# Moving the preparation of latent attention's weights into the opening block of the layer before it

## The chip, the cores and the metric

One Trainium2 chip, one of its cores, with its five engines: TensorE (PE), VectorE (DVE), ScalarE (ACT), GpSimd (POOL) and SyncE (SP), which issues the DMAs. The metric is the device time of one execution in microseconds; lower is better. TensorE's clock is granted at one of two levels, 1.2 or 2.4 GHz; the profile gives it as a share of the upper one.

## The reference

Eight sequences of 512 tokens, 256 wide, go through six sub-layers: an expert feed-forward, a small attention, the expert feed-forward again, a routed layer, latent attention, and the routed layer again. Cut to the two that matter here:

```python
# latent attention: B=8, L=512, D=256, 16 heads of 64, latent 64
x_bld = layernorm(x)
q = einsum('bld,dhk->blhk', x_bld, Wq)
latent = einsum('bld,dc->blc', x_bld, Wkv_down)
k = einsum('blc,chk->blhk', latent, Wk_up)
v = einsum('blc,chk->blhk', latent, Wv_up)
attn = softmax(where(causal, einsum('bqhd,bkhd->bhqk', q, k) / sqrt(64), neg_inf))
x = x + einsum('bqhd,hdo->bqo', einsum('bhqk,bkhd->bqhd', attn, v), Wout)

# routed layer: 64 tokens of each sequence, by the router's weight, 63 of them kept
weights = (layernorm(x) @ router_w)[..., 0] + router_b[0]
topv, topi = top_k(weights, 64); sel_idx = sort(topi[:, :63])
# the chosen tokens go through rmsnorm, rope, attention with a mask, a feed-forward
out = zeros_like(x).at[bidx, sel_idx].set(proc)
x = x + 0.5 * (out + layernorm(x) * (1.0 - sel_mask)[..., None])
```

## The kernel before

`macaron_kernel` calls four layer functions one after the other; x (all tokens, 128 partitions) and the identity matrix stay in SBUF between them. Each layer is a row of blocks; a block is one instruction stream per engine, and all engines meet at its end. `layer` clears the layer's semaphores, one by one on SyncE, in a block of its own after each layer.

`routed_layer` (tag routed1 or routed2) has an opening block and a main block. In the opening block SyncE issues three small loads (router row, router bias, position rows; `small_in`) and nine loads of weights (`weights_in`). VectorE goes through statistics of 32 tiles (L982), the layernorm's columns (`layernorm_columns`, L81 to L61), 32 weighings (L992: x less its mean times the router's row, summed into `w_col`), and waits for TensorE to turn `w_col` into rows (L1055, `rows_turned`). Then it picks the 64 largest of each sequence in 8 rounds (L1017, L1019), numbers them (L1026 to L1044), and copies them back after another turn by TensorE (L1061) to `slot_col` and `stay` (L1046, L1047). ScalarE writes the normalized tokens `y`, 32 tiles in 8 batches (L1072), from when `shift` is there (L985). GpSimd writes a few constants. In the main block TensorE gathers the chosen tokens from `y` with one-hot matrices (L1208), and the layer goes on.

`latent_attention_layer` has two blocks. The first prepares weights. SyncE loads Wk_up, Wv_up, Wq, Wout and Wkv_down (L1681 to L1685); TensorE turns the first three (L1708, L1714) and VectorE copies the turned ones to SBUF (L1751, L1754). Then for each of 8 pairs of heads TensorE multiplies Wq with Wk_up (L1727) and Wv_up with Wout (L1730), so that the layer can work on the latent directly. Each product is needed as a sum of two float16 tiles: ScalarE writes the upper part (`b_hi` L1780, `a_hi` L1781) and VectorE the rest (`b_lo` L1768, `a_lo` L1770), straight from PSUM. GpSimd makes constants, and VectorE fills tiles whose unused rows must be 0 or 1 (L1742 to L1748). The second block is the attention: `stream` walks a pipeline over batches and heads; its first steps are the layernorm of the first batch, with statistics on VectorE (L74), the variance on GpSimd (L111 to L124), the start of the reciprocal root on VectorE (L49), Newton steps on GpSimd (L131 to L137), the normalized tiles on VectorE (L102), then turns on TensorE (L1969).

The order of the work is written out by hand, in each engine's stream; waits name counts of semaphores.

## Time and profile before

| | us |
|---|---|
| median of the runs | 2927.89 (2927.53 to 2929.93, 3 runs) |
| the profiled execution | 2929.78, its span 2928.0 |
| TensorE busy | 2487.5 (85%) |
| VectorE busy | 2105.5 (72%) |
| ScalarE busy | 1570.2 (54%) |
| GpSimd busy | 843.4 (29%) |

The page also divides the span into 40 slices of 73.2 us; a digit is the busy share in tenths (for PEclk, the granted clock). The first expert and attention layers take the first 21 slices and a half; the first routed layer runs from 1585 to 1782 us, latent attention from 1786 to 2717, the second routed layer from there.

```profile
## 2 busy tenths in 40 slices
PE   6999999999999999989995567588888888897276
PEld 3444444444444444444442355255555555564164
DVE  3479688878979896888512754589778878974754
ACT  5655454645555554546553251277667766765241
POOL 3444343444444443435442100002112211212000
PEclk9999999999999999999998766699999999998577
```

The 22nd to 26th digits are the routed layer and the start of latent attention: the lowest digits of TensorE but for the ends, and the lowest clock but for the last layer. Times in the rows further down are microseconds from the start of the span.

### The profile page before, as it was taken

What the parts mean: (1) busy time and instruction counts of PE and PEld (TensorE: products, weight loads), DVE (VectorE), ACT (ScalarE), POOL (GpSimd) and SP (SyncE); (2) the same over time, 40 slices, a digit from 0 to 9 for tenths busy, and PEclk for the clock granted to TensorE, in tenths of its full rate; (3) what the DMA queues carried; (4) which work ended last, traced back from release to release, by engine and by line L of the source; (5) the groups of instructions that cost most, each with busy time, mean ns of one, the idle gap of its engine ahead of it and who ended that gap; (6) DMA issues with size and microseconds to landing.
All of it is one profiled execution on the core that took longest, in us unless ns stands there. A gap on an engine that the chain in (4) does not pass through costs nothing. (4 is left out here: it accounts for less than half of the span.)

```text
span 2928.0 us, 39722 instructions
## 1 busy us (share of the span) xinstructions
PE 2487.5 (85%) x14369; PEld 1353.9 (46%) x14369; DVE 2105.5 (72%) x3904; ACT 1570.2 (54%) x2517; POOL 843.4 (29%) x816
## 2 busy tenths in 40 slices
PE   6999999999999999989995567588888888897276
PEld 3444444444444444444442355255555555564164
DVE  3479688878979896888512754589778878974754
ACT  5655454645555554546553251277667766765241
POOL 3444343444444443435442100002112211212000
PEclk9999999999999999999998766699999999998577
DMA  5000000000000000000001001000000000000101
GB/s 165 26 1 1 1 1 1 1 1 1 1 1 1 1 1 1 1 1 1 1 1 49 15 1 37 0 2 2 2 2 2 2 3 2 2 2 2 49 16 58
DMA packets 29477, 33.24 MB, mean 11 GB/s; under 512 B 6568, under 2 KB 25704, under 8 KB 29272
## 3 DMA queue, kind: packets, MB, share of 16 engines
q1 hardware_dynamic: 28296, 28.02, 3.0%
q0 software_dynamic: 976, 2.56, 0.3%
q8 instruction: 120, 1.97, 0.3%
q14 instruction: 85, 0.70, 0.1%
HBM read 25.72 MB, written 4.19 MB: 10 GB/s over the span
## 5 line engine op out<-in xcount | busy, mean ns | idle before, releaser
L716 POOL TENSOR_TENSOR g_lo<-g_full,g_hi 128x512 f16<-128x512 f32 x512 | 658.7, 1290 | 910.3 <-ACT g_hi L788 908.6
L788 ACT ACTIVATE g_full<-hid,b_col 128x512 f32<-128x512 f32 x512 | 351.6, 687 | 559.5 <-PE hid L152 558.1
L150 PE MATMUL hid<-y_hi,w_hi 128*128 128x512 f16 x1024 | 396.1, 387 | 37.6 <-DVE y_lo L774 34.9
L151 PE MATMUL hid<-y_lo,w_hi 128*128 128x512 f16 x1024 | 395.3, 386 | 0.0
L152 PE MATMUL hid<-y_hi,w_lo 128*128 128x512 f16 x1024 | 394.8, 386 | 0.0
L150 PE MATMUL acc<-g_hi,w_hi 128*128 128x512 f16 x1024 | 388.9, 380 | 0.0
L151 PE MATMUL acc<-g_lo,w_hi 128*128 128x512 f16 x1024 | 388.9, 380 | 0.0
L152 PE MATMUL acc<-g_hi,w_lo 128*128 128x512 f16 x1024 | 388.6, 379 | 0.0
L788 ACT ACTIVATE g_hi<-hid,b_col 128x512 f16<-128x512 f32 x512 | 349.0, 682 | 0.0
L2048 DVE TENSOR_REDUCE mla_m_col<-mla_ps 128x1 f32<-128x512 f32 (+3 forms) x512 | 224.9, 483 | 62.4 <-PE mla_ps L1890 56.6
L2151 ACT ACTIVATE mla_p_full<-mla_ps 128x1280 f32<-128x1280 f32 x128 | 158.4, 1237 | 140.0 <-PE mla_ps L1920 139.6
L2129 DVE TENSOR_TENSOR mla_p_lo<-mla_p_full,mla_p_hi 128x1280 f16<-128x1280 f32 x128 | 205.4, 1605 | 2.9 <-ACT mla_p_hi L2151 2.4
L2188 POOL TENSOR_TENSOR mla_o_lo<-mla_o,mla_o_hi 128x512 f16<-128x512 f32 x64 | 106.5, 1670 | 324.8 <-ACT mla_o_hi L2160 324.8
L1889 PE MATMUL mla_ps<-mla_key_hl,mla_q_hi 128*128 128x512 f16 (+3 forms) x512 | 130.4, 308 | 70.5 <-DVE mla_m_col L2048 69.7
L677 DVE TENSOR_TENSOR prod<-score,v_rows 128x1024 f32<-128x1024 f32 x128 | 178.5, 1394 | 3.0
L150 PEld LDWEIGHTS hid<-y_hi,w_hi 128*128 128x128 f16 x1024 | 101.5, 99 | 161.7 <-DVE y_lo L774 38.8
L640 DVE TENSOR_TENSOR prod<-qk_rot 128x1024 f32<-128x1024 f32 x128 | 173.2, 1353 | 3.3
L1916 PE MATMUL mla_ps<-mla_q_hi,mla_key_hl 128*128 128x512 f16 (+3 forms) x512 | 156.6, 306 | 8.2 <-issue 6.7
L152 PEld LDWEIGHTS hid<-y_hi,w_lo 128*128 128x128 f16 x1024 | 101.8, 99 | 125.6 <-issue 8.6
L679 DVE TENSOR_REDUCE o_rows<-prod 128x64 f32<-128x1024 f32 x128 | 156.1, 1220 | 4.4
L643 DVE TENSOR_REDUCE score<-prod 128x64 f32<-128x1024 f32 x128 | 156.1, 1220 | 4.4
L2151 ACT ACTIVATE mla_p_hi<-mla_ps 128x1280 f16<-128x1280 f32 x128 | 157.6, 1231 | 0.0
(366 smaller groups left out, 4823.8 us busy)
## 6 DMA issues: line engine op xcount, KB each, us to landing
stage<-in_L_ffn_w_dram SPq DMA_DIRECT2D x16, 512.0 KB, 4.8
x<-in_L_attn_x_dram SPq DMA_DIRECT2D x8, 512.0 KB, 8.4
routed_w<-in_L_ffn_w_dram SPq DMA_DIRECT2D x4, 1024.0 KB, 8.2
out_dram<-x SPq DMA_DIRECT2D x8, 512.0 KB, 4.5
mla_sums<-mla_sum_row SPq DMA_DIRECT2D x128, 2.0 KB
mla_wq<-in_L_attn_Wq_dram SPq DMA_DIRECT2D x1, 1024.0 KB, 7.3
mla_wout<-in_L_attn_Wout_dram SPq DMA_DIRECT2D x1, 1024.0 KB, 8.6
routed_wqkv<-in_L_ffn_wq_dram SPq DMA_DIRECT2D x2, 256.0 KB, 3.7
```

The source lines that it names most:

```text
L150: pe.matmul(out, w_hi, v_hi, start=first, stop=False)
L151: pe.matmul(out, w_hi, v_lo, start=False, stop=False)
L152: return pe.matmul(out, w_lo, v_hi, start=False, stop=final)
L640: dve.tensor_tensor(pr, q4, k4, ALU.mult).then_inc(head_step, 1)
L643: dve.tensor_reduce(score[:, row:row + GROUP, :], pr, AX.X, ALU.add).then_inc(head_step, 1)
L677: dve.tensor_tensor(pr, e4, v4, ALU.mult).then_inc(head_step, 1)
L716: pool.tensor_tensor(g_lo[:, g, :], g_full[:, g, :], g_hi[:, g, :], ALU.subtract).then_inc(tail_done, 1)
L788: act.activation(out[:, g, :], hid[:, ht % 4, :], ACT.Gelu, bias=b1_col[:, ht:ht + 1], scale=1.0 / WS).then_inc(gelu_done, 1)
L1916: pe.matmul(flat[:, at:at + cols], key_hl[:, (slot + (h + 1) // H) % 2, toks], q_hi[:, hh % RING, t * P:], start=True, stop=False)
L2048: dve.tensor_reduce(m_col[:, g % 2, t, j:j + 1], flat[:, QUERY_AT[t]:QUERY_AT[t] + (t + 1) * P], AX.X, ALU.max).then_inc(s_max, 1)
L2129: dve.tensor_tensor(p_lo[:, hh % 2, :], p_full[:, hh % 2, :], p_hi[:, hh % 2, :], ALU.subtract).then_inc(p_tail, 1)
L2151: act.activation(out[:, hh % 2, :], flat[:, 3 * 512:3 * 512 + KEY_COLS], ACT.Exp, scale=float(MLA_DIM) ** -0.5).then_inc(exp_done, 1)
```

## The change

The tiles that latent attention's weights end in (`LatentWeights`) are now allocated ahead of the first routed layer and outlive it. Loading, turning, folding and splitting (`LatentFold`) stand in the opening block of that layer (only of the first; the second gets no `latent`), and the first block of latent attention is gone.

- SyncE issues the five loads after the three small ones and ahead of the nine loads of routed weights.
- TensorE turns the weights and folds the first four pairs behind the turn of the position rows, ahead of the turn of `w_col`; the other four pairs stand between that turn and the turn of the picked rows. It uses PSUM banks 3 to 7, two for each pair in turn, where it had all eight.
- ScalarE copies the turned weights to SBUF (VectorE did) and copies each product whole, in float32, to `a_full` and `b_full`. Turned weights and the first four pairs stand ahead of the first normalized tile, the other four ahead of those of batches 1, 3, 5 and 7.
- GpSimd makes the constants, with their casts (VectorE did those), splits Wkv_down, and splits each pair from SBUF: two copies to float16 and two subtractions of 256 elements a partition. VectorE takes no part in the fold.
- The fills of unused rows move to latent attention's remaining block (`set_tiles`), behind the statistics of the first batch; TensorE and SyncE wait for them at their start.
- To make room, in both routed layers `p_t` lies on `mask_rows`, `o` and `o_t` on `mask_t`, and `proc` on half of `s`.

```diff
--- before.py
+++ after.py
...
+class LatentFold:
...
+    def load(self, sp):
+        io = self.to.io
+        sp.dma_start(self.wk[:, :], io["Wk_up"].rearrange("c h n -> c (h n)")).then_inc(self.k_in, 16)
+        sp.dma_start(self.wv[:, :], io["Wv_up"].rearrange("c h n -> c (h n)")).then_inc(self.v_in, 16)
+        sp.dma_start(self.wq[:, :, :], io["Wq"].rearrange("(k p) h n -> p k (h n)", p=P)).then_inc(self.q_in, 16)
+        sp.dma_start(self.wout[:, :, :], io["Wout"].rearrange("(m h) n d -> (h n) m d", h=2)).then_inc(self.out_in, 16)
+        sp.dma_start(self.down[:, :, :], io["Wkv_down"].rearrange("(k p) c -> p k c", p=P)).then_inc(self.down_in, 16)
+
+    def turn(self, pe):
+        ps, first = self.ps, self.FIRST_BANK
+        for i, (w, there) in enumerate(((self.wk, self.k_in), (self.wv, self.v_in))):
+            pe.wait_ge(there, 16)
+            for m in range(MLA_PAIRS):
+                last = pe.transpose(ps[:, first + i, m * LATENT:(m + 1) * LATENT], w[:, m * P:(m + 1) * P],
+                                    self.ident[0:LATENT, 0:LATENT])
+            last.then_inc(self.turned, 1)
+        pe.wait_ge(self.q_in, 16)
+        for m in range(MLA_PAIRS):
+            if m == 6:
+                pe.wait_ge(self.turn_out, 1)
+            bank = first + (2, 3, 4, 0)[m // 2]
+            for k in range(KD):
+                at = (m % 2) * D + k * P
+                last = pe.transpose(ps[:, bank, at:at + P], self.wq[:, k, m * P:(m + 1) * P], self.ident[:, :])
+            if m % 2 == 1:
+                last.then_inc(self.turned, 1)
+
+    def bank(self, m, i):
+        return self.FIRST_BANK + 2 * (m % 2) + i
+
+    def folded_a(self, m, i):
+        return self.ps[:, self.bank(m, i), 0:KD * LATENT].rearrange("p (k c) -> p k c", k=KD)
+
+    def fold(self, pe, m):
+        if m == 0:
+            pe.wait_ge(self.out_in, 16)
+            pe.wait_ge(self.turn_out, 6)
+        if m >= 2:
+            pe.wait_ge(self.fold_out, m - 1)
+        for i in range(2):
+            bank = self.bank(m, i)
+            rows = slice(i * MLA_DIM, (i + 1) * MLA_DIM)
+            for k in range(KD):
+                pe.matmul(self.ps[:, bank, k * LATENT:(k + 1) * LATENT], self.wq_t[rows, m, k * P:(k + 1) * P],
+                          self.wk_t[rows, m, :], start=True, stop=True)
+            last = pe.matmul(self.ps[i * LATENT:(i + 1) * LATENT, bank, D:2 * D], self.wv_t[rows, m, :],
+                             self.wout[rows, m, :], start=True, stop=True)
+        last.then_inc(self.folded, 1)
+
+    def turned_copies(self, act):
+        for i, w in enumerate((self.wk_t, self.wv_t)):
+            act.wait_ge(self.turned, i + 1)
+            act.activation(w[:, :, :].rearrange("p m c -> p (m c)"), self.ps[:, self.FIRST_BANK + i, :],
+                           ACT.Copy).then_inc(self.turn_out, 1)
+        for n in range(4):
+            act.wait_ge(self.turned, n + 3)
+            act.activation(self.wq_t[:, 2 * n:2 * n + 2, :].rearrange("p m d -> p (m d)"),
+                           self.ps[:, self.FIRST_BANK + (2, 3, 4, 0)[n], :], ACT.Copy).then_inc(self.turn_out, 1)
+
+    def folded_copies(self, act, m):
+        act.wait_ge(self.folded, m + 1)
+        if m >= 2:
+            act.wait_ge(self.split_step, 4 * (m - 1))
+        for i in range(2):
+            rows = slice(i * LATENT, (i + 1) * LATENT)
+            act.activation(self.b_full[rows, m % 2, :], self.ps[rows, self.bank(m, i), D:2 * D], ACT.Copy, scale=WS)
+            last = act.activation(self.a_full[:, m % 2, :, i, :], self.folded_a(m, i), ACT.Copy, scale=WS)
+        last.then_inc(self.fold_out, 1)
+
+    def constants(self, pool):
+        to, made = self.to, self.made
+        for i, value in enumerate(NORM_CONSTANTS):
+            pool.memset(to.norm_const[:, i, :], value)
+        pool.memset(self.spread_f[:, :, :], 0.0).then_inc(made, 1)
+        pool.memset(self.block_f[:, :, :], 0.0).then_inc(made, 1)
+        for n, base in enumerate((0, -32)):
+            pool.wait_ge(made, 2 + n)
+            pool.affine_select(out=self.spread_f[:, :, :], in_=self.spread_f[:, :, :], compare_op=ALU.not_equal,
+                               fill=1.0 / INV_SCALE, base=base, pattern=[[-1, MLA_HEADS], [0, LATENT]],
+                               channel_multiplier=1).then_inc(made, 1)
+        pool.affine_select(out=self.block_f[:, 0, :], in_=self.block_f[:, 0, :], compare_op=ALU.is_ge, fill=BLOCKED,
+                           base=0, pattern=[[-1, P]], channel_multiplier=1).then_inc(made, 1)
+        pool.affine_select(out=self.block_f[:, 1, :], in_=self.block_f[:, 1, :], compare_op=ALU.is_ge, fill=BLOCKED,
+                           base=0, pattern=[[1, P]], channel_multiplier=-1).then_inc(made, 1)
+        pool.wait_ge(made, 6)
+        pool.tensor_copy(to.spread[:, :, :], self.spread_f[:, :, :])
+        pool.tensor_copy(to.block_q[:, :], self.block_f[:, 0, :])
+        pool.tensor_copy(to.block_k[:, :], self.block_f[:, 1, :])
+        pool.tensor_copy(to.ident_b[:, :], self.ident[:, :])
+        pool.wait_ge(self.down_in, 16)
+        pool.tensor_scalar(self.down[:, :, :], self.down[:, :, :], WS, None, ALU.mult).then_inc(self.down_step, 1)
+        pool.wait_ge(self.down_step, 1)
+        for i in range(2):
+            pool.tensor_copy(to.down_hi[:, :, i, :], self.down[:, :, :]).then_inc(self.down_step, 1)
+        pool.wait_ge(self.down_step, 3)
+        for i in range(2):
+            pool.tensor_tensor(to.down_lo[:, :, i, :], self.down[:, :, :], to.down_hi[:, :, i, :], ALU.subtract)
+
+    def split(self, pool, m):
+        to, slot = self.to, m % 2
+        a_hi, a_lo = (w[:, :, 2 * m:2 * m + 2, :] for w in (to.a_hi, to.a_lo))
+        pool.wait_ge(self.fold_out, m + 1)
+        pool.tensor_copy(a_hi, self.a_full[:, slot, :, :, :]).then_inc(self.split_step, 1)
+        pool.tensor_copy(to.b_hi[:, m, :], self.b_full[:, slot, :]).then_inc(self.split_step, 1)
+        pool.wait_ge(self.split_step, 4 * m + 2)
+        pool.tensor_tensor(a_lo, self.a_full[:, slot, :, :, :], a_hi, ALU.subtract).then_inc(self.split_step, 1)
+        pool.tensor_tensor(to.b_lo[:, m, :], self.b_full[:, slot, :], to.b_hi[:, m, :],
+                           ALU.subtract).then_inc(self.split_step, 1)
...
@@ -937,6 +1123,9 @@
             pick_step = tsem("pick_step")
             cols_turned = tsem("cols_turned")
 
+            fold = LatentFold(nc, part, tsem, ps, ident, latent) if latent is not None else None
+            FOLDS_EARLY = MLA_PAIRS // 2
+
             COLUMNS_AT = ALL_TILES + LN_COLUMN_STEPS
             MASK_BATCHES = 4
             idx_row = row[:, 0, :]
@@ -951,6 +1140,8 @@
 
                     sp.dma_start(pos_rows[:, :], io["position_ids"][:, 0:SEQ].rearrange("b (t p) -> b t p", p=P)
                                  ).then_inc(small_in, 16)
+                    if fold is not None:
+                        fold.load(sp)
                     for i, name in enumerate(("wq", "wk", "wv")):
                         sp.dma_start(wqkv[:, :, i * D:(i + 1) * D], io[name].rearrange("(k p) n -> p k n", p=P)).then_inc(weights_in, 16)
                     sp.dma_start(wo[:, :, :], io["wo"].rearrange("(k p) n -> p k n", p=P)).then_inc(weights_in, 16)
@@ -972,6 +1163,10 @@
                         pool.iota(y[:, b, :, D + 2], pattern=[[P, TILES]], base=min(b, MASK_BATCHES - 1) * 1024,
                                   channel_multiplier=1, allow_small_or_imprecise_dtypes=True).then_inc(made, 1)
                     pool.memset(y[:, :, :, D + 3], 0.0).then_inc(made, 1)
+                    if fold is not None:
+                        fold.constants(pool)
+                        for m in range(MLA_PAIRS):
+                            fold.split(pool, m)
 
                 @block.vector
                 def _(dve):
@@ -1050,10 +1245,17 @@
                 def _(pe):
                     pe.wait_ge(col_out, 1)
                     pe.transpose(ps[:, 1, 0:16], pos_rows_f[:, :], ident[0:16, 0:16]).then_inc(cols_turned, 1)
+                    if fold is not None:
+                        fold.turn(pe)
+                        for m in range(FOLDS_EARLY):
+                            fold.fold(pe, m)
                     pe.wait_ge(weigh_step, ALL_TILES + 2)
                     for t in range(TILES):
                         last = pe.transpose(ps[0:BATCH, 0, t * P:(t + 1) * P], w_col[:, :, t], ident[:, :])
                     last.then_inc(rows_turned, 1)
+                    if fold is not None:
+                        for m in range(FOLDS_EARLY, MLA_PAIRS):
+                            fold.fold(pe, m)
                     pe.wait_ge(pick_step, 2 + 2 * (ROWS // 8) + 9)
                     for i, r in ((0, 5), (1, 3)):
                         for t in range(TILES):
@@ -1065,8 +1267,14 @@
                 @block.scalar
                 def _(act):
 
+                    if fold is not None:
+                        fold.turned_copies(act)
+                        for m in range(FOLDS_EARLY):
+                            fold.folded_copies(act, m)
                     act.wait_ge(norm_step, COLUMNS_AT + 1)
                     for b in range(BATCH):
+                        if fold is not None and b % 2 == 1:
+                            fold.folded_copies(act, FOLDS_EARLY + b // 2)
                         for t in range(TILES):
                             col = TILES * b + t
                             act.activation(y[:, b, t, 0:D], x[:, b, t, :], ACT.Identity, bias=shift[:, col:col + 1],
@@ -1089,13 +1297,13 @@
         v_blk = sb("v_blk", [P, BATCH, 8, 2, HEAD_DIM])
         s = sb("s", [P, 2, HEADS, ROWS])
         s_col = sb("s_col", [P, 2, 3, HEADS])
-        p_t = sb("p_t", [P, 2, 8, P])
-        o = sb("o", [P, 2, D])
-        o_t = sb("o_t", [P, 2, KD, P])
+        p_t = mask_rows[:, :, :].rearrange("p r n -> p (r n)").rearrange("p (a m n) -> p a m n", a=2, m=8)
+        o = mask_t[:, 0, :, :].rearrange("p t n -> p (t n)").rearrange("p (a d) -> p a d", a=2)
+        o_t = mask_t[:, 1, :, :].rearrange("p t n -> p (t n)").rearrange("p (a k n) -> p a k n", a=2, k=KD)
         x1 = sb("x1", [P, PAIRS, D])
 
         gel = qk_t[:, :, :, :].rearrange("p r a n -> p (r a n)").rearrange("p (f n) -> p f n", f=FFN // P)
-        proc = sb("proc", [P, PAIRS, D])
+        proc = s[:, 0, :, :].rearrange("p h c -> p (h c)").rearrange("p (r d) -> p r d", r=PAIRS)
         proc_hi = sb("proc_hi", [P, PAIRS, D], F16)
         proc_lo = sb("proc_lo", [P, PAIRS, D], F16)
 
...
-def latent_attention_layer(nc, keep, x, ident, io):
+def latent_attention_layer(nc, keep, x, ident, latent):
...
@@ -1807,6 +1843,7 @@
         inv = sb("inv", [P, SEQ // SUM_ROWS])
         inv_part = sb("inv_part", [P, 2, SEQ // SUM_ROWS], F16)
 
+        zeroed = sem("zeroed")
         norm_step = sem("norm_step")
         y_turned = sem("y_turned")
         y_split = sem("y_split")
@@ -2048,6 +2085,17 @@
             dve.tensor_reduce(m_col[:, g % 2, t, j:j + 1], flat[:, QUERY_AT[t]:QUERY_AT[t] + (t + 1) * P],
                               AX.X, ALU.max).then_inc(s_max, 1)
 
+        def set_tiles(dve):
+
+            dve.memset(key_top[LATENT:P, :, :], 0.0).then_inc(zeroed, 1)
+            for slot in range(2):
+                dve.memset(val_hi[:, slot, :, LATENT:P], 1.0)
+                dve.memset(val_lo[:, slot, :, LATENT:P], 0.0)
+            dve.wait_ge(zeroed, 1)
+            dve.memset(key_top[LATENT:LATENT + 1, :, :], M_SCALE)
+            dve.memset(q_lo[LATENT:P, :, :], 0.0)
+            dve.memset(inv_hl[:, :], 0.0).then_inc(zeroed, 1)
+
         def vector_step(dve, b, slot, h):
             before, after = b - 1, b + 1
             other_bank = PV_BANK[(h + 1) % 2]
@@ -2081,6 +2129,8 @@
 
             if exists(after) and h == NORM_AT:
                 layernorm_stats(dve, norm_step, x[:, after, :, :], stats)
+                if isinstance(b, int) and after == 0:
+                    set_tiles(dve)
             if exists(after) and h == GUESS_AT:
                 rsqrt_start(dve, norm_step, NORM_STEPS * after + TILES + VARIANCE_STEPS, var[:, :], rstd[:, :])
             if exists(after) and h == APPLY_AT:
@@ -2208,6 +2258,7 @@
         with nc.Block() as block:
             @block.tensor
             def _(pe):
+                pe.wait_ge(zeroed, 2)
                 stream(pe, tensor_step)
 
             @block.vector
@@ -2224,6 +2275,7 @@
 
             @block.sync
             def _(sp):
+                sp.wait_ge(zeroed, 2)
                 stream(sp, dma_step)
 
 
@@ -2278,8 +2330,10 @@
                             sp.sem_clear(semaphore)
 
         layer(expert_and_head_layers, x, ident, experts)
-        layer(routed_layer, "routed1", x, ident, routed)
-        layer(latent_attention_layer, x, ident, latent)
+        with ExitStack() as lasting:
+            weights = LatentWeights(nc, lasting, latent)
+            layer(routed_layer, "routed1", x, ident, routed, None, weights)
+            layer(latent_attention_layer, x, ident, weights)
         layer(routed_layer, "routed2", x, ident, routed, out)
 
 
```

## Rows read from the trace of the kernel before

**Rows 1.** windows: length, busy us (count) by engine, granted clock, DMA share, GB/s
```profile
1585.60:1640.20 54.60, 2.32 (x13) 1.45 (x13) 46.48 (x158) 15.84 (x32) 1.88 (x12) 0.50 0.20 66
...
1805.00:1830.00 25.00, 25.00 (x74) 14.50 (x73) 8.00 (x24) 7.20 (x25) 0.00 (x0) 0.50 0.00 1
...
1836.00:1850.00 14.00, 2.26 (x9) 1.47 (x10) 4.51 (x12) 1.20 (x2) 4.17 (x22) 0.50 0.00 1
```

**Rows 2.** timeline, start and length in us: between the layers, first statistics
```profile
1778.88 3.48 DVE L1517 SCALAR_TENSOR_TENSOR x<-routed_ps,x 128x1024 f32<-128x1024 f32 x3
...
1785.78 0.55 SPq L1681 DMA_DIRECT2D mla_wk<-in_L_attn_Wk_up_dram  x1
...
1836.11 1.40 DVE L74 BATCH_NORM_STATS2 mla_stats<-x 128x6 f32<-128x256 f32 x4 [0.32 <-PEq L1678]
```

**Rows 3.** timeline of the routed layer's opening block, by engine
```profile
1587.40 0.39 SPq L955 DMA_DIRECT2D routed_wqkv<-in_L_ffn_wq_dram  x1
...
1604.82 15.84 ACT L1072 ACTIVATE routed_y<-x,routed_shift,routed_rstd 128x256 f32<-128x256 f32 x32 [24.32 <-DVE routed_shift L985]
...
1618.34 1.02 PE L1055 MATMUL routed_ps<-ident,routed_w_col 128*8 128x128 f32 x4 [27.50 <-DVE routed_w_col L999]
...
1639.90 0.18 DVE L1047 COPY routed_stay<-routed_ps 128x32 f32<-128x32 f32 x1
```

**Rows 4.** timeline of the fold's block, and Wout's landing from the DMA view
```profile
1794.33 3.43 PE L1714 MATMUL mla_ps<-ident,mla_wq 128*128 128x128 f32 x16 [1.28 <-DMA mla_wq<-in_L_attn_Wq_dram]
...
1800.28 0.63 PE L1727 MATMUL mla_ps<-mla_wk_t,mla_wq_t 64*128 64x64 f32 x4 [2.52 <-DVE mla_wq_t L1754]
...
1804.07 0.38 ACT L1780 ACTIVATE mla_b_hi<-mla_ps 64x256 f16<-64x256 f32 x1 [45.58 <-PE mla_ps L1730]
...
1808.22 0.38 ACT L1780 ACTIVATE mla_b_hi<-mla_ps 64x256 f16<-64x256 f32 x1 [2.94 <-PE mla_ps L1730]
...
mla_wout<-in_L_attn_Wout_dram SPq DMA_DIRECT2D x1, 1024.0 KB, 8.6
```

**Rows 5.** ScalarE's groups by form, 1600 to 1836: busy, mean ns
```profile
L1780 ACT ACTIVATE mla_b_hi<-mla_ps 64x256 f16<-64x256 f32 x16 | 6.0, 378 | 66.3 <-PE mla_ps L1730 66.2
...
L1781 ACT ACTIVATE mla_a_hi<-mla_ps 128x128 f16<-128x128 f32 x16 | 4.3, 268 | 0.1
...
L1527 ACT ACTIVATE routed_h_t<-routed_ps 128x512 f32<-128x512 f32 x4 | 2.2, 594 | 14.0 <-PE routed_ps L1406 14.0
```

**Rows 6.** GpSimd: one line (ns min/median/max), then groups by form (mean ns)
```profile
L716 POOL TENSOR_TENSOR g_lo<-g_full,g_hi x512: 1148/1157/2225, 31.1 to 1575.4; 128x512 f16<-128x512 f32 x171
...
L1695 POOL TENSOR_SCALAR_AFFINE_SELECT mla_spread_f<-mla_spread_f 128x1024 f32<-128x1024 f32 x2 | 2.3, 1147 | 0.3
...
L113 POOL TENSOR_TENSOR mla_ln_col<-mla_stats 128x4 f32<-128x4 f32 x8 | 1.6, 203 | 0.0
...
L1698 POOL TENSOR_SCALAR_AFFINE_SELECT mla_block_f<-mla_block_f 128x128 f32<-128x128 f32 x1 | 0.3, 293 | 0.0
```

**Rows 7.** VectorE beside GpSimd: timeline near 297, three lines (ns min/median/max)
```profile
297.33 2.46 POOL L716 TENSOR_TENSOR g_lo<-g_full,g_hi 128x512 f16<-128x512 f32 x2 [6.42 <-ACT g_hi L788]
...
297.40 3.35 DVE L625 TENSOR_TENSOR rot<-qk,rope 128x256 f32<-128x256 f32 x4
...
L625 DVE TENSOR_TENSOR rot<-qk,rope x128: 411/418/1378, 152.2 to 1344.9; 128x256 f32<-128x256 f32 x128
...
L643 DVE TENSOR_REDUCE score<-prod x128: 1219/1220/1221, 156.7 to 1356.8; 128x64 f32<-128x1024 f32 x128
...
L992 DVE SCALAR_TENSOR_TENSOR routed_weighed<-x,routed_ln_col,routed_router x64: 469/480/484, 1604.7 to 2751.9; 128x256 f32<-128x256 f32 x64
```

**Rows 8.** VectorE's timeline: first and last fill, then its wait for the variance
```profile
1791.39 0.27 DVE L1742 MEMSET mla_val_hi<- 128x256 f16 x1
...
1795.53 0.91 DVE L1748 MEMSET mla_key_top<- 1x1024 f16 x1 [0.27 <-DVE mla_key_top L1746]
...
1839.72 0.17 DVE L49 TENSOR_SCALAR mla_rstd<-mla_var 128x4 int32<-128x4 int32 x1 [2.20 <-POOL mla_minus_half L124]
```

219 lines of the change are left out of this document (63 added, 156 removed).

## The prediction

> **What bounds the kernel now.** I read the change first (it touches one stretch of the program and moves it), then the table of windows for that stretch and for the one it is moved into, then the timeline of both by engine, and last the rows that show what GpSimd costs VectorE. Latent attention opens with a block of its own that loads, turns, folds and splits its weights. It starts at 1785.8 us and the first useful instruction of the layer, the layernorm's statistics, starts at 1836.11 [rows 2]: 50.3 us in which no token is touched. TensorE bounds it: it is busy throughout from 1805 to 1830, with ScalarE and VectorE mostly idle, at a granted clock of 0.50, the lower level of 1.2 GHz [rows 1]; a pair of heads comes out every 4.16 us [rows 4]. The opening block of the first routed layer is the opposite: of its 54.6 us VectorE is busy for 46.5, TensorE for 2.3, GpSimd for 1.9 [rows 1]. VectorE's order there is the path: statistics, 32 weighings, a turn by TensorE, 8 rounds of picking; ScalarE's 32 normalized tiles end at 1620.7, far ahead of the end at 1640.1 [rows 3].
>
> **The sum, part by part.**
>
> *The block that goes: -50.3 us.* Nothing in the next block can start sooner than the removed one did (1785.78) and it started at 1836.11 [rows 2]. The semaphores are cleared between the layers, in the 3.4 us from 1782.36 to 1785.78 [rows 2]; the fold's twelve are now cleared one layer earlier, so that cancels.
>
> *Its loads.* They are queued behind the three small ones that VectorE waits for and ahead of the nine routed weights. SyncE reaches that place at 1587.40 [rows 3]. Before, the turn of Wq started at 1794.33 [rows 4], 8.55 us after the first issue at 1785.78 [rows 2], and Wout had landed 11.5 us after it (issue 2.9 us later, 8.6 us to landing [rows 4]). So: turn of Wq at 1596.0, Wout there at 1598.9. The nine routed loads are issued about 4.4 us later and land some 8 us later; they are waited for only after the selection, beyond 1650: nothing.
>
> *TensorE, early half.* The turn of Wq takes 3.43 us [rows 4], so it ends at 1599.4; ScalarE (instead of VectorE) empties the last bank 0.6 us later [rows 5]: 1600.1. The first pair takes 3.8 us and each further one 4.16 [rows 4]: folded at 1603.9, 1608.1, 1612.2 and 1616.4. Behind these on TensorE stands the turn of the router's column, which was ready at 1618.3 [rows 3]: 1.9 us to spare, so early folds are hidden. ScalarE needs 2 x 0.378 + 2 x 0.268 = 1.29 us a pair [rows 5], so its copies are out at 1605.2, 1609.4, 1613.5, 1617.7. Only then does it start the 32 normalized tiles (0.495 us each, 1.98 a batch) that began at 1604.8 before [rows 3].
>
> *GpSimd's splits.* No GpSimd copy of this shape is in the trace. A subtraction takes 1.157 us for 512 elements and 0.20 for 4 [rows 6], so 0.68 for 256. A one-input pass takes 1.147 us for 1024 and 0.293 for 128 [rows 6], so 0.41 for 256; bounds are the fixed part of a short instruction, 0.20, and the subtraction's 0.68; I take 0.41, the nearest kind (it too reads one operand). One pair is 2 x 0.41 + 2 x 0.68 = 2.2 us, within the 4.16 of a fold. The page GPSIMD Engine Reference of the Trainium skill (section Elementwise, side-by-side cycle accounting) gives about 1.03 cycles an element for light bodies and 2.6 for `tensor_tensor`. At its 1.2 GHz that is an estimate of 0.22 and 0.55 us for 256 elements, 1.5 us a pair as the part that streams; by it four splits would cost VectorE 6.2 us instead of 5.6 and the sum would read 2889.8.
>
> *What the splits cost VectorE.* This is the dear part. At 297.33 two GpSimd subtractions run back to back, and the VectorE instructions of the same time, which take 0.41 us alone, take up to 1.38; four take 3.35 us instead of about 1.4 [rows 7]. That is 2 us for two subtractions: each holds VectorE for about 0.97 us, its own 1.16 less 0.19. VectorE's reductions, which read one operand, never stretch (1219 to 1221 ns in 128 of them) [rows 7]. The 32 weighings read two operands from SBUF (x and the router's row), like those that stretch; alone they take 0.48 [rows 7]. So a split costs VectorE 2.2 - 4 x 0.19 = 1.4 us if it falls among them. They start at 1604.7 [rows 7] and end 0.5 us ahead of the column's turn at 1618.3 [rows 3], at 1617.8; splits start at 1605.2, 1609.4, 1613.5 and, as the first three stretch the weighing to about 1622, also 1617.7. That is 4 x 1.4 = 5.6 us, and about 0.5 for GpSimd's five small instructions on the down projection, which meet the short two-operand ones at 1601 to 1604.6. Together 6.1. From both sides: nothing if the weighings don't share what the rotations share; 12 us if a copy costs a subtraction and the whole duration is held (4 x 2.7 + 1.2).
> The page Advanced Engine Details and Errata of the Trainium skill (section Mode Summary) says that GpSimd and two-port VectorE instructions block each other, and names only the fast modes; a float32 instruction on two tensors is none of those, and by that narrow rule the 6.1 us would be 0 (the first rival). The stretched rotations are float32 on two tensors, so the trace speaks against the narrow reading.
>
> *The late half.* The router's column is ready at 1618.3 + 6.1 = 1624.4, turned 1.1 us later (1.02 of work [rows 3]) at 1625.5; the fifth pair is folded at 1629.7. From there ScalarE is the bound: by its order only the first batch of tiles can go ahead; then come 4 x 1.29 of copies and 7 x 1.98 of tiles, 19.1 us: 1648.8. GpSimd's last split, beside the last batch, ends at 1649.0. VectorE's own path ends at 1640.1 + 6.1 + 1.4 (one split among the last two-operand steps) = 1647.6. The block thus ends at 1649.0 instead of 1640.1: +8.9 us, of which 2.8 would stand without any contention (1618.3 + 1.1 + 4.2 + 19.1 + 0.2 = 1642.9).
>
> *Latent attention's start: +2.7 us.* VectorE now fills its tiles right behind the statistics. Those fills took from 1791.39 to 1796.44, 5.05 us with 0.27 of idle time ahead of the last [rows 8]. Before, VectorE went on 2.20 us after its statistics, once GpSimd's variance was there [rows 8]; now at the end of the fills, about 4.9 us. Fills read nothing, so I let GpSimd's variance run beneath them; bounds +2.2 (that gap gone, and as much again where the fills change partitions) and +4.8 (variance only after them). TensorE and SyncE wait for the fills too, but their first work needs the normalized tiles, which are later still. The clock is at 0.50 at the layer's start before [rows 1], and TensorE is idle ahead of it after as well: nothing.
>
> *The aliases* (p_t, o, o_t, proc on tiles that are dead by then) bring no wait and no instruction: nothing.
>
> Sum: -50.3 + 8.9 + 2.7 = **-38.7 us**. The profiled execution took 2929.78 us (span 2928.0), the three timed ones 2927.9 in the median; the difference applied to the median gives **2889.2 us**.
>
> **The rivals.**
> 1. *No contention.* The weighings run at their own pace: -50.3 + 2.8 + 2.7 = -44.8, 2883.1 us. For it: nothing measured on this very instruction with GpSimd active; against: the rotations [rows 7].
> 2. *Dearer splits.* A GpSimd copy costs as much as a subtraction and whole durations are held: 12 + 2.8 + 0.5 in the opening, +3.4 at the start: -31.6, 2896.3 us. For it: the missing copy row.
> 3. *Late loads, so the fold isn't hidden.* The turn of the router's column stands behind four folds on TensorE. With 6.1 us of contention the slack is 8 us; loads 12 us later than reckoned would push the block by 4 more, 2893 us. Against: only the three small loads stand ahead of them.
> 4. *Slower than before.* One mechanism: GpSimd's chain of eight splits becomes the bound of the opening block. It begins at 1605.2; for the whole gain of 47.6 us to be lost, 8 splits must end at 1687.7, 10.3 us a split or 2.6 us an instruction, against 0.68 reckoned. At 11 us a split the kernel takes 2933.5. The longest subtraction of 512 elements that waited for VectorE took 2.2 us [rows 6], so this needs worse than the worst row on each.
>
> **How the numbers follow.** Likeliest case 0.56, its own range 2885 to 2893 (0.9 to 2.0 us held a split, fills +2.2 to +3.4); rival 1 0.17; rival 2 0.15; rival 3 0.07; rival 4 0.02; and 0.03 that something unseen gives back so much that the result is within 0.2%, about what a measurement of this kernel can tell from no change. The range of 2880 to 2898 takes in rivals 1 and 2. Faster 0.95, same 0.03, slower 0.02.
>
> **What would show it.** In the profile after: statistics of latent attention start about 3.5 us after the routed layer's last instruction; weighings of up to 1 us instead of 0.48, and their 32 over some 18.7 us instead of 13.1; the turn of the router's column near 1624.4 with TensorE idle before it; normalized tiles on ScalarE in batches, the last near 1649; the gap between statistics and the reciprocal root's start 4.9 instead of 2.2 us. Unstretched weighings prove rival 1; GpSimd copies of 0.6 us and more, rival 2; a turn of the router's column that follows the fourth fold without idle time, rival 3. The prediction is wrong if TensorE's clock is at its upper level in the folds (about 2 us less) or if the later layers change.

## The result and the profile after

| | us, median of its runs | runs, lowest to highest |
|---|---|---|
| before | 2928.34 | 4 runs, 2927.53 to 2929.93 |
| after | 2885.94 | 4 runs, 2884.84 to 2888.88 |

The ratio is 0.9853, 95% interval 0.9841 to 0.9864: 42.4 us less, with 2889.2 forecast and 2880 to 2898 as range. The profiled execution of after took 2884.84 us (span 2882.7).

The opening block of the first routed layer, from the table of windows of after (length, busy us and count of PE, PEld, DVE, ACT, POOL, granted clock, DMA share, GB/s), answers to the first row of [rows 1]:

```profile
1587.20:1648.30 61.10, 41.55 (x141) 25.87 (x141) 51.86 (x158) 28.48 (x70) 29.92 (x66) 0.50 0.32 103
```

It is 6.5 us longer. VectorE has the same 158 instructions and 5.4 us more of busy time: the same instructions take longer, because they meet GpSimd's (contention; splits_after below takes it away again). TensorE now works for 41.55 us of the block, at the same lower level of the clock.

The timeline of after at the change of layers (start, length, engine, line, operation, count, in brackets the idle time before and what ended it) answers to [rows 2] and [rows 8]:

```profile
1785.52 2.35 DVE L1725 SCALAR_TENSOR_TENSOR x<-routed_ps,x 128x1024 f32<-128x1024 f32 x2
1792.02 1.41 DVE L74 BATCH_NORM_STATS2 mla_stats<-x 128x6 f32<-128x256 f32 x4 [4.16 <-PEq L2326]
1793.51 0.20 POOL L111 TENSOR_TENSOR mla_ln_col<-mla_stats 128x4 f32<-128x4 f32 x1 [132.72 <-DVE mla_stats L74]
1793.59 0.48 DVE L2090 MEMSET mla_key_top<- 64x512 uint32 x1 [0.16 <-issue]
...
1795.38 0.20 POOL L124 TENSOR_TENSOR mla_minus_half<-mla_var,mla_norm_const 128x4 f32<-128x4 f32 x1
1796.55 1.76 DVE L2096 MEMSET mla_q_lo<- 64x2048 uint32 x1 [0.38 <-issue]
1798.42 0.27 DVE L2097 MEMSET mla_inv_hl<- 128x256 uint32 x1
1798.61 0.11 DVE L49 TENSOR_SCALAR mla_rstd<-mla_var 128x4 int32<-128x4 int32 x1
```

From the last addition to x (ends at 1787.87) to the statistics it was 53.76 us and is 4.15. The block is gone whole. The clearing of semaphores, which stands in this gap, has grown, as the line view of the clearings shows (ns min/median/max), first of before, then of after:

```profile
L2278 SPq EVENT_SEMAPHORE_RANGE_CLEAR  x51: 25/29/30, 1782.6 to 1785.5; - x51
```

```profile
L2330 SPq EVENT_SEMAPHORE_RANGE_CLEAR  x63: 25/29/34, 1788.1 to 1791.7; - x63
```

Twelve more clearings, 0.057 us from one start to the next, are 0.7 us. GpSimd's variance (ready at 1795.58) runs beneath the fills at its usual 0.20 us an instruction, and VectorE starts the reciprocal root 3.0 us after it is there.

TensorE in the opening block of after, from its timeline (compare [rows 3, 4]):

```profile
1598.88 3.68 PE L975 MATMUL routed_ps<-ident,fold_wq 128*128 128x128 f32 x16 [3.63 <-DMA fold_wq<-in_L_attn_Wq_dram]
1603.33 1.08 PE L995 MATMUL routed_ps<-fold_wk_t,fold_wq_t 64*128 64x64 f32 x4 [0.78 <-ACT fold_wq_t L1008]
...
1624.26 1.02 PE L1254 MATMUL routed_ps<-ident,routed_w_col 128*8 128x128 f32 x4 [4.25 <-DVE routed_w_col L1194]
```

The first fold starts 16.2 us after the block's first load was issued (1587.13), 1.8 us later than forecast. The four early folds are nevertheless done 4.25 us before the router's column is ready, so VectorE still sets when that turn starts.

Below is the timeline of VectorE and GpSimd in after, beside the first split (the reads of VectorE's accumulator that stand between the weighings are left out):

```profile
1608.86 0.68 POOL L1054 CAST mla_a_hi<-fold_a_full 128x256 f16<-128x256 f32 x1 [3.82 <-ACT fold_a_full L1018]
1609.21 0.61 DVE L1187 SCALAR_TENSOR_TENSOR routed_weighed<-x,routed_ln_col,routed_router 128x256 f32<-128x256 f32 x1
1609.48 0.59 POOL L1055 CAST mla_b_hi<-fold_b_full 128x256 f16<-128x256 f32 x1
1609.75 0.60 DVE L1187 SCALAR_TENSOR_TENSOR routed_weighed<-x,routed_ln_col,routed_router 128x256 f32<-128x256 f32 x1
1610.16 0.72 POOL L1057 TENSOR_TENSOR mla_a_lo<-fold_a_full,mla_a_hi 128x256 f16<-128x256 f32 x1
1610.28 0.88 DVE L1187 SCALAR_TENSOR_TENSOR routed_weighed<-x,routed_ln_col,routed_router 128x256 f32<-128x256 f32 x1
1610.84 0.84 POOL L1058 TENSOR_TENSOR mla_b_lo<-fold_b_full,mla_b_hi 128x256 f16<-128x256 f32 x1
1611.09 0.88 DVE L1187 SCALAR_TENSOR_TENSOR routed_weighed<-x,routed_ln_col,routed_router 128x256 f32<-128x256 f32 x1
1611.90 0.47 DVE L1187 SCALAR_TENSOR_TENSOR routed_weighed<-x,routed_ln_col,routed_router 128x256 f32<-128x256 f32 x1
```

A weighing takes 0.48 us alone [rows 7]. Beside a cast it takes 0.60 and beside a subtraction 0.88. The next one starts 0.54 and 0.81 us later instead of 0.41. So a cast (GpSimd's copy to float16) holds VectorE for 0.13 us, a subtraction for 0.40, and a split (two of each) for 1.06.

The end of the block, from the timelines of ScalarE and GpSimd in after:

```profile
1640.65 4.03 ACT L1280 ACTIVATE routed_y<-x,routed_shift,routed_rstd 128x256 f32<-128x256 f32 x8
1644.58 0.36 ACT L1017 ACTIVATE fold_b_full<-routed_ps 64x256 f32<-64x256 f32 x1
...
1645.68 2.06 ACT L1280 ACTIVATE routed_y<-x,routed_shift,routed_rstd 128x256 f32<-128x256 f32 x4
...
1647.29 0.67 POOL L1058 TENSOR_TENSOR mla_b_lo<-fold_b_full,mla_b_hi 128x256 f16<-128x256 f32 x1
1648.27 1.80 POOL L1591 MEMSET routed_v_blk<- 128x2048 f32 x1 [0.31 <-POOLq L1134]
```

ScalarE works without a gap, 5.03 us for a pair and two batches of tiles. Its last tile ends at 1647.74 and GpSimd's last split at 1647.96. VectorE's last copy had ended at 1646.76. ScalarE's order ends the block, and GpSimd follows it.

Single executions of one kernel lie up to 6 us from their median. Differences of 1 to 5 us are therefore read in stages of the traces. Each number below, in us, is worked out from the starts and ends of instructions in one trace. The opening runs from GpSimd's first instruction in the block to the first one of the main block; the column's turn is its start, the last tile its end; the gap is that between the last addition to x and the first statistics:

| trace | opening | 32 weighings, first to last start | column's turn, from the opening's start | last tile, from the same | routed main block | gap to the statistics | end of statistics to reciprocal root |
|---|---|---|---|---|---|---|---|
| before | 54.67 | 12.61 | 32.67 | 34.98 | 142.01 | 53.76 | 2.21 |
| before_again | 54.44 | 12.60 | 32.44 | 34.75 | 143.05 | 54.21 | 2.20 |
| after | 61.11 | 16.11 | 37.11 | 60.59 | 139.60 | 4.15 | 5.19 |
| again | 61.32 | 17.05 | 37.31 | 60.79 | 143.02 | 4.15 | 5.19 |
| after_same_chip | 61.28 | 16.25 | 37.26 | 60.75 | 139.47 | 4.16 | 5.19 |
| splits_after | 59.16 | 12.60 | 33.11 | 58.63 | 144.09 | 4.15 | 5.19 |
| tiles_early | 60.41 | 16.92 | 37.35 | 58.23 | 140.36 | 4.15 | 5.19 |
| fills_spread | 61.35 | 16.96 | 37.35 | 60.82 | 139.45 | 4.15 | 2.19 |
| doubled | 65.44 | 20.74 | 41.41 | 64.90 | 142.15 | 4.15 | 5.19 |
| casts_doubled | 62.16 | 17.86 | 38.15 | 61.63 | 142.40 | 4.16 | 5.19 |
| loads_last | 64.30 | 14.05 | 40.27 | 63.77 | 142.37 | 4.15 | 5.19 |
| combined | 55.85 | 12.60 | 32.73 | 53.61 | 144.01 | 4.15 | 2.20 |
| combined_same_chip | 56.05 | 12.61 | 32.94 | 53.82 | 141.24 | 4.15 | 2.20 |

The column of the main block is there as a warning. The change does nothing to its instructions but place some of its tiles elsewhere (the aliases), and it spreads over 4.6 us, from 139.5 to 144.1 among kernels that have the same main block.

### The profile page after: what moved, and what is told of

Same layout as the page of the kernel before. It is cut to its first block and busy times, and to the rows that moved or that the text cites. A ratio compares the mean times of both kernels' runs of the same rounds, so it can differ in the third digit from the quotient of the medians.

```text
span 2882.7 us, 39721 instructions
## 1 busy us (share of the span) xinstructions
PE 2486.1 (86%) x14369; PEld 1352.4 (47%) x14369; DVE 2096.4 (73%) x3859; ACT 1572.1 (55%) x2523; POOL 866.9 (30%) x857
```

## The experiments

**The changed kernel again.** The main block of the first routed layer was 2.4 us shorter in after than in before. Is that the change's doing?

> The changed kernel once more, unedited, beside the kernel before on this chip. It measured 42.4 us less in the medians where 38.7 were forecast. Theory A: the terms of the change add up to about 40.9 (49.6 gone between the layers, 6.4 more in the opening block, 3.0 more behind the statistics, 0.7 given back where fewer semaphores are cleared), and what is beyond is the spread between executions: the routed layer's main block, 2.4 us shorter in the first profile, comes out anywhere between 139.5 and 142.5 us, and the ratio moves towards 0.986. Theory B: the fold lifts TensorE's clock earlier in the main block: its first products (64 of them, 11.4 us before) again take 9.9 us, the main block is again near 139.6 us, and the ratio stays at 0.985 or below.

Main block 143.02 us, a little above the range of theory A; 2888.03 us (4 runs) beside 2931.08 of before on that chip, ratio 0.9854, 0.9837 to 0.9870. The 2.4 us are spread between executions. The first 64 products took 10.45 us, and 10.46 in before_again, not the 9.9 of theory B. The rows of windows for this block, the first of after and the second of again, show what goes with it:

```profile
1648.30:1787.90 139.60, 106.30 (x808) 78.61 (x808) 78.04 (x218) 48.69 (x184) 7.43 (x6) 0.79 0.03 8
```

```profile
1648.40:1791.40 143.00, 110.46 (x808) 80.81 (x808) 78.12 (x218) 48.58 (x184) 7.47 (x6) 0.75 0.03 8
```

The work is the same (808 products in both) and the mean granted clock is 0.79 in one and 0.75 in the other.

**The kernel before again**, to see the same from the other side.

> The kernel before, unedited, for a second trace of it. Theory A (the routed layer's main block varies by execution): its length is not again 142.0 us but anywhere from 139.5 to 144 us, as in the five traces of kernels that have the same main block; the opening block is again 54.7 us and the stretch from the layer's last instruction to the statistics 53.8. Theory B (the main block is shorter after the change): 142 us or more here.

Main block 143.05 us, opening 54.44, gap 54.21: before also has long main blocks. With two traces of before, neither of them below 142, theory B is not ruled out by this run; again, where the changed kernel has 143.02, speaks against it. The stages around the change repeat to 0.5 us. 2932.04 us (one run).

**Splits held back until the weighings are over.**

```diff
                         fold.constants(pool)
+                        pool.wait_ge(weigh_step, ALL_TILES)
                         for m in range(MLA_PAIRS):
                             fold.split(pool, m)
```

> GpSimd starts its first split only when the 32 weighings are done; nothing else is changed. Theory A (a GpSimd instruction that reads SBUF holds the weighings): the 32 weighings take 13.0 us from first to last start plus one, as before the change, instead of 16.9; the turn of the router's column is 4.2 us sooner; ScalarE's third pair waits for the first split, so the block ends only some 2.9 us sooner than in the changed kernel: 0.9990 of its time. Theory B (the stretch comes from ScalarE's and TensorE's own SBUF traffic in the same time): weighings of up to 0.88 us stay, in the places where pairs are folded, and nothing moves.

The line view of the weighings (ns min/median/max), first of after (the first routed layer), then of splits_after (both routed layers):

```profile
L1187 DVE SCALAR_TENSOR_TENSOR routed_weighed<-x,routed_ln_col,routed_router x32: 474/481/881, 1606.4 to 1622.5; 128x256 f32<-128x256 f32 x32
```

```profile
L1188 DVE SCALAR_TENSOR_TENSOR routed_weighed<-x,routed_ln_col,routed_router x64: 475/480/484, 1607.1 to 2712.3; 128x256 f32<-128x256 f32 x64
```

No weighing is stretched any more (longest 484 ns instead of 881), and their 32 starts take 12.60 us as in before. The turn comes 4.0 to 4.2 us sooner. In this run TensorE still folded four pairs and ScalarE copied two of them beside the weighings, so neither of these stretched them: GpSimd is the cause, shown. The block ends only 2.0 to 2.2 us sooner (2.9 expected), because with two slots ScalarE now waits for the late splits, 9.73 us ahead of the third pair:

```profile
1622.51 0.38 ACT L1017 ACTIVATE fold_b_full<-routed_ps 64x256 f32<-64x256 f32 x1 [9.73 <-POOL mla_b_lo L1058]
```

The whole kernel took 2889.09 us, ratio 0.9861 (0.9844 to 0.9877): 2 us are below what this comparison can tell.

**Tiles between the early copies.**

```diff
                         fold.turned_copies(act)
-                        for m in range(FOLDS_EARLY):
-                            fold.folded_copies(act, m)
+                        fold.folded_copies(act, 0)
                     act.wait_ge(norm_step, COLUMNS_AT + 1)
                     for b in range(BATCH):
-                        if fold is not None and b % 2 == 1:
-                            fold.folded_copies(act, FOLDS_EARLY + b // 2)
+                        if fold is not None and b > 0:
+                            fold.folded_copies(act, b)
```

> ScalarE's order is changed alone: one batch of normalized tiles behind each pair from the first on, so that four batches lie between the early folds instead of behind the turn of the router's column. Theory A (ScalarE bounds the late half, VectorE is about 1.2 us behind it): ScalarE's last tile ends near 1645 instead of 1647.7, the last split sooner by as much, and the block then ends with VectorE's copies, 0.5 to 1.2 us sooner than in the changed kernel. Theory B (TensorE's late folds, every 4.16 us, bound it): no change, the last split keeps its place behind the eighth pair.

The last tile ends 2.4 to 2.6 us sooner and the block only 0.7 to 0.9, since VectorE's copies (60.15 us after the start) are now last. The two bounds lay about 1 us apart, so either edit alone can win little. 2886.84 us, ratio 0.9857 (0.9841 to 0.9874).

**The fills spread.** The row of ones, the zeros of q_lo and of inv_hl are written behind the start of the reciprocal root, while GpSimd runs its Newton steps.

```diff
+        def set_more_tiles(dve):
             dve.wait_ge(zeroed, 1)
             dve.memset(key_top[LATENT:LATENT + 1, :, :], M_SCALE)
...
                 rsqrt_start(dve, norm_step, NORM_STEPS * after + TILES + VARIANCE_STEPS, var[:, :], rstd[:, :])
+                if isinstance(b, int) and after == 0:
+                    set_more_tiles(dve)
```

> Only the first five fills stay behind the statistics; the other three (2.9 us) go behind the start of the reciprocal root, where VectorE waits 3.4 us for GpSimd's Newton steps. Theory A (the fills cost what VectorE is late for the variance, 5.2 instead of 2.2 us): the wait between statistics and reciprocal root is 2.2 us again, the normalized tiles start some 3.5 us behind it as before, and the kernel is 2.9 us faster than the changed one. Theory B (GpSimd's small instructions wait while VectorE fills, so that moving the fills moves the delay): the Newton steps stretch from 3.4 to 5 us or more and less than 1 us is gained.

VectorE's timeline in fills_spread:

```profile
1795.41 0.17 DVE L49 TENSOR_SCALAR mla_rstd<-mla_var 128x4 int32<-128x4 int32 x1 [0.59 <-POOL mla_minus_half L124]
...
1796.05 0.91 DVE L2097 MEMSET mla_key_top<- 1x1024 f16 x1 [0.27 <-issue]
...
1799.20 0.27 DVE L2099 MEMSET mla_inv_hl<- 128x256 uint32 x1
1799.39 1.19 DVE L102 TENSOR_SCALAR mla_y<-x,mla_ln_col,mla_rstd 128x256 f32<-128x256 f32 x4
```

VectorE waits for the variance again, as before the change, and the gap is 2.19 us instead of 5.19. The later fills end 0.4 us behind GpSimd's Newton steps (their last ends at 1799.11, at its usual 0.20 us a step): from the start of the reciprocal root to the normalized tiles it is 3.98 instead of 3.67. 2.7 us are gained in this stage, 2.9 were expected. 2885.40 us, ratio 0.9852 (0.9835 to 0.9868).

**Every early split done twice.** The second casts and subtractions go into a tile that nobody reads.

```diff
+        self.again = sb("again", [P, MLA_PAIRS // 2, 4, D], F16)
...
         pool.tensor_copy(to.b_hi[:, m, :], self.b_full[:, slot, :]).then_inc(self.split_step, 1)
+        flat_a = self.a_full[:, slot, :, :, :].rearrange("p k i c -> p (k i c)")
+        for i, w in enumerate((flat_a, self.b_full[:, slot, :])):
+            if m < MLA_PAIRS // 2:
+                pool.tensor_copy(self.again[:, m, i, :], w)
         pool.wait_ge(self.split_step, 4 * m + 2)
+        for i, w in enumerate((flat_a, self.b_full[:, slot, :])):
+            if m < MLA_PAIRS // 2:
+                pool.tensor_tensor(self.again[:, m, 2 + i, :], w, to.b_hi[:, m, :], ALU.subtract)
```

> In the first four pairs GpSimd does each of the four instructions of a split twice, the second time into a tile that nothing reads. Theory A (each GpSimd instruction that reads SBUF holds one weighing for the time it streams, whatever else goes on): from the first doubled split on, GpSimd is never idle during the weighings; there a weighing takes 0.67 us on average instead of 0.41; from first to last start they take some 19.1 us instead of 17.0, and the turn of the router's column is 2.2 us later. Theory B (what delays the weighings is the ScalarE copy or the TensorE product that comes with each pair): still 17.0 us.

The turn came 4.1 us later than in again, and the weighings took 20.74 us: the direction is right, the expected size (2.2 us) too small. Eight casts of 0.13 and eight subtractions of 0.40 are 4.2 us, so the prices read from the first split hold. Of the 4.1 us, 3.7 are in the weighings and 0.4 in the short two-operand steps ahead of them, which the first split now meets. 2890.21 us (one run).

**Only the casts done twice** (the same edit without its second half), to price the two kinds apart.

> The two casts of each of the first four pairs are done once more, into a tile that nobody reads; the subtractions are left as they are. Theory A (a GpSimd instruction holds VectorE for a time of its own kind: 0.13 us a cast, 0.40 a subtraction, as the starts of the weighings in the changed kernel's trace say): eight more casts, 1.1 us, weighings from first to last start 18.1 us instead of 17.05, weighings beside casts at 0.60, and turn of the router's column about 1 us later. Rival B (what is held is a share of GpSimd's busy time, whatever it does: 4.45 us for the four splits of 2.6 us each, that is 0.43 of it): eight casts of 0.59 us hold 2.0 us, weighings 19.1 us.

VectorE and GpSimd beside the second split of casts_doubled:

```profile
1611.29 0.40 POOL L1055 CAST mla_a_hi<-fold_a_full 128x256 f16<-128x256 f32 x1 [0.54 <-ACT fold_a_full L1019]
1611.37 0.60 DVE L1192 SCALAR_TENSOR_TENSOR routed_weighed<-x,routed_ln_col,routed_router 128x256 f32<-128x256 f32 x1
1611.64 0.59 POOL L1056 CAST mla_b_hi<-fold_b_full 128x256 f16<-128x256 f32 x1
1611.90 0.60 DVE L1192 SCALAR_TENSOR_TENSOR routed_weighed<-x,routed_ln_col,routed_router 128x256 f32<-128x256 f32 x1
```

Weighings 17.86 us and the turn 0.8 us later than in again: theory A (18.1), not B (19.1). What is held is not one share of GpSimd's busy time. Whether it is a matter of the instruction's kind is not shown: both prices are also the undisturbed length less 0.27 us (0.40 and 0.13, 0.67 and 0.40), and no run changes the length of one kind. 2888.84 us (one run).

**The fold's loads behind the nine routed ones** (`fold.load(sp)` moved below the load of inv_freq).

> The five loads of the fold are issued behind the nine of the routed weights. Theory A (the early folds are hidden only while they end before the weighings; the slack is 4.2 us): the turn of Wq starts some 8 us later, the fourth pair is folded at about 40.9 us from the block's start, and the turn of the router's column, ready near 34, follows it without idle time on TensorE at 40.8 instead of 37.3; the opening block grows by 3.5 us. At the same time only one or two splits meet the weighings, which take 14 us or less. Theory B (the order of the loads is free): the opening block stays at 61.3 us.

TensorE in loads_last:

```profile
1607.59 3.28 PE L975 MATMUL routed_ps<-ident,fold_wq 128*128 128x128 f32 x16 [1.25 <-DMA fold_wq<-in_L_attn_Wq_dram]
...
1626.62 1.02 PE L1254 MATMUL routed_ps<-ident,routed_w_col 128*8 128x128 f32 x4
```

There is no idle time ahead of the column's turn: it stands behind the fourth fold, 3.0 us later than in again, although the weighings are shorter (14.05, fewer splits meet them). The block is 3.0 us longer (3.5 expected). This is rival 3, brought about by the order of the loads. 2894.27 us (one run).

**All three cures together**: splits after the weighings, tiles between the early copies, fills spread, and four slots instead of two, so that ScalarE doesn't wait.

```diff
...
-        self.a_full = sb("a_full", [P, 2, KD, 2, LATENT])
-        self.b_full = sb("b_full", [P, 2, D])
+        self.a_full = sb("a_full", [P, 4, KD, 2, LATENT])
+        self.b_full = sb("b_full", [P, 4, D])
...
-        if m >= 2:
-            act.wait_ge(self.split_step, 4 * (m - 1))
+        if m >= 4:
+            act.wait_ge(self.split_step, 4 * (m - 3))
...
```

> Splits behind the weighings, a batch of tiles behind each pair, and the fills spread, together; a_full and b_full get four places each, so that ScalarE can go on with the third and fourth pair before the first split. Theory A (the three terms are separate, and with ScalarE's and GpSimd's chains shortened VectorE bounds the block again): the opening block of the routed layer takes about 57.2 us from its first instruction to the main block's (61.3 in the changed kernel, 54.7 before), 21.7 of them behind the turn of the router's column plus two splits (2.1) that meet the last two-operand steps; the statistics wait 2.2 us; together 6.9 us less than the changed kernel. Theory B (GpSimd bounds it: eight splits in a row from the end of the weighings on): the last split ends 1 us or more behind VectorE's copies and the opening stays above 58.5 us.

The opening takes 55.85 us (57.2 expected), 1.2 us more than in before, with the whole fold inside it. The late splits do meet the end of the picking, in VectorE's timeline of combined:

```profile
1638.28 1.57 DVE L1234 TENSOR_TENSOR_SCAN routed_row<-routed_row 8x512 f32<-8x512 f32 x1
...
1641.05 0.88 DVE L1240 TENSOR_SCALAR routed_row<-routed_w_row,routed_best 8x512 f32<-8x512 f32 x1
```

They cost about 1.1 us, where two splits at the price beside the weighings would be 2.1: from the column's turn to VectorE's last copy it is 22.86 us instead of 21.74. And the early folds are nearly the bound again: without stretched weighings TensorE's idle time ahead of the column's turn is 3.40 us in combined, 0.94 in splits_after and 0.47 in combined_same_chip. 2880.37 us (5 runs) beside 2928.42 of before, ratio 0.9833 (0.9820 to 0.9847).

**After and combined on one chip**, since the two had been timed on different ones.

> The changed kernel once more, unedited, on the same chip as the combined version, five rounds. Expected from its eight earlier times (2884.5 to 2891.8 us): a median of 2887, 0.985 to 0.986 of the kernel before. If the combined version is really better by its stages, this one is 6 to 8 us slower than it here; if the difference so far was one between chips, they come within 2 us.

> The combined version once more, unedited, beside the changed kernel on the same chip, five rounds. By the stages of its first trace: opening 5.4 us shorter, fills 2.7 us: 8 us off 2887, so 2879, ratio 0.983 of the kernel before. Rival: the stages are given back later (routed1's main block 144 instead of 139.6 to 143 us), then 2884 to 2886.

| | median us | lowest to highest | ratio to before (2927.03) |
|---|---|---|---|
| after_same_chip | 2885.26 | 2882.70 to 2890.14 (4) | 0.9862, 0.9847 to 0.9877 |
| combined_same_chip | 2880.70 | 2876.06 to 2883.18 (5) | 0.9837, 0.9823 to 0.9850 |

Combined is 4.6 us below after here, and 6.2 us in the mean of all executions (2880.55 over 10, 2886.77 over 12), give or take 2.5 by their spread. The stages say 5.2 to 5.4 in the opening and 2.7 at the fills, about 8. It beats both kernels. The missing 2 to 3 us are within the spread of single executions, and the runs don't say whether they are given back.

## Why the prediction was right, point by point

**The block that goes: right.** -50.3 forecast; the gap shrank by 49.6. The other 0.7 us is the clearing of the fold's twelve semaphores, which moved to this place (63 clearings instead of 51). It comes back at the end of latent attention, where there are 36 instead of 48: from the last addition to x to the next layer's first instruction it is 2.52 us in all eleven traces with the change and 3.17 in both of before. So it does cancel, as forecast.

**The loads: up to 1.4 us too early.** In after Wq was turned 11.7 us after the block's start instead of 10.4. In the nine other traces with this order of loads it was 10.1 to 11.3, so it spreads between executions, and no run shows by what. It cost nothing, as the fold had 4.25 us to spare, and loads_last shows where that ends.

**GpSimd's splits: right in price.** Where nothing meets them, from GpSimd's timeline of after:

```profile
1631.10 0.40 POOL L1055 CAST mla_b_hi<-fold_b_full 128x256 f16<-128x256 f32 x1
1631.58 0.67 POOL L1057 TENSOR_TENSOR mla_a_lo<-fold_a_full,mla_a_hi 128x256 f16<-128x256 f32 x1
```

0.40 and 0.67, with 0.41 and 0.68 interpolated from other shapes.

**Contention: right mechanism, term too large.** The step that was mis-sized reads "each holds VectorE for about 0.97 us, its own 1.16 less 0.19", carried over to casts and to 256 elements as duration less 0.19: 0.22 a cast and 0.49 a subtraction. They are 0.13 and 0.40: what had to be taken off was 0.27 and not 0.19, which came from subtractions of 512 elements beside the rotations (0.96 of 1.16 us held there). So a split costs 1.06 us and not 1.4, the four 4.2 and not 5.6; the down projection cost about 0.4 instead of 0.5. Together 4.6 against 6.1; the turn came 4.4 us later from the block's start than in before. Rival 1 (nothing) falls by the weighings of 0.88 us and by splits_after. Rival 2 (dearer) falls by casts of 0.40. The narrow reading, in the prediction, of Advanced Engine Details and Errata of the Trainium skill (section Mode Summary), by which only the fast modes are blocked, doesn't hold here: the weighings are float32 on two tensors and were held. The page GPSIMD Engine Reference of the Trainium skill (section Key points) names contention also with VectorE instructions that have two SBUF inputs. By that rule the weighings should suffer, and the trace agrees: 0.88 us instead of 0.48.

**ScalarE's late half: right.** Period 5.03 us against 5.25, since copies and tiles overlap by some hundredths each; 18.3 us against 19.1 (the forecast's own terms add up to 19.0). The block grew by 6.4 us instead of 8.9. Of the 2.5 us, 1.6 are the column's turn, at 37.1 us after the start (forecast 38.7), which is the smaller contention, and 0.8 are the shorter period. The order of what is late was right: ScalarE, then GpSimd's last split 0.2 us behind it, then VectorE.

**The fills: right.** +3.0 against +2.7, and undone by fills_spread. The variance did run beneath them.

**The sum: right to 2.2 us, the rest not explained.** The terms that the prediction named measure -49.6 - 0.7 (the clearings) + 6.4 + 3.0 = -40.9, forecast -38.7; of the 2.2 us the opening holds 2.5, less 0.3 at the fills. The medians differ by 42.4, the means over all chips by 41.8 (2928.59 over 29 executions of before, 2886.77 over 12 of after). What is beyond 40.9 lies in stages whose instructions the change leaves alone. The two profiled executions are 45.3 us apart (spans 2928.0 and 2882.7), and their stages add up to that: +1.5 ahead of the routed layer, +6.4 the opening, -2.4 the main block, -49.6 the gap, +2.9 from the statistics to the normalized tiles, -1.4 the rest of latent attention, -0.7 the clearings, -2.0 the second routed layer.

**The signs of being wrong** that the prediction named did show, both of them in part. The later layers changed. From the first normalized tile to latent attention's last addition it is 873.6 and 873.7 us in the two traces of before, and 871.2 to 876.1 with the change, median 872.2. From the second routed layer's first instruction to the end it is 207.8 and 207.7 in before; with the change it is 205.8 to 206.1 in nine traces and 208.0 and 208.2 in two. Nine of the eleven lie below both traces of before. But two traces are few, and the aliases, which touch that layer too, were never run by themselves: their "nothing" is not shown. And the clock rose during the early folds in four of the eleven traces with the change (after_same_chip, doubled, loads_last, combined). The row of windows of combined there:

```profile
1600.00:1605.00 5.00, 4.22 (x22) 2.96 (x21) 4.76 (x20) 1.97 (x4) 1.92 (x5) 0.84 1.09 373
```

The granted clock is 0.84 there and 0.50 in the same window of after. From the first fold to the end of the fourth it is 14.7 to 15.0 us in these four traces and 16.7 in the others: 2 us less, as forecast. Except in loads_last, where the turn stands right behind the folds, that time is hidden.

**The slower rival** needed splits of over 10 us. They took 2.1 to 3.9.

## What to carry to other kernels

A block that bounds the time by one engine while the others idle can be moved under a block bound by another engine, and then costs only what the two share: here 50.3 us became 9.4. Price it by the waits that come last in the new place, and look at the second-latest too: two bounds lay 1 us apart, and each cure of the opening alone won 1 to 2 us where both, with four slots, won 5.3. Put GpSimd's work beside VectorE instructions that it doesn't hold (here the rounds of picking, not the weighings), and put fills into the time in which VectorE waits for another engine's short chain.

## What the runs showed of the hardware that I had not expected

- What a GpSimd instruction takes from a VectorE instruction on two SBUF operands is less than its own length: 0.13 us for a cast of 256 elements (0.40 long) and 0.40 for a subtraction of 256 (0.67 long) beside weighings, 0.96 for a subtraction of 512 (1.16 long) beside rotations. The length less 0.27, 0.27 and 0.20 us: whether kind or length sets it stays open.
- It is mutual: in after casts stretch from 0.40 to 0.59 (one to 0.68) and subtractions from 0.67 to 0.72 and 0.84 beside weighings, and to 0.92 and 1.46 beside the last steps of the picking.
- A one-operand instruction can be held too. VectorE's scaling of the picked row (8 x 512 float32) took 0.41 us in before and 0.78 beside a subtraction, from VectorE's timeline of after:

```profile
1644.19 0.78 DVE L1238 TENSOR_SCALAR routed_row<-routed_row 8x512 f32<-8x512 f32 x1
```

  The rounds of picking (0.68 and 0.66 us), which also read one operand, never were, nor the reductions of [rows 7], although 104 of the 128 overlap a subtraction of GpSimd in the trace of before. VectorE's fills neither slowed GpSimd's small instructions (0.20 us each) nor were slowed by them (0.48, 0.27, 0.17 and 0.91 us, as in before).
- A block of the same 808 products takes between 139.5 and 144.1 us in thirteen traces, with a mean granted clock of 0.79 to 0.75: the same order as most effects studied here.
